# Two layers of attention and experts on one core: router logits and gate values of layer 1 projected in transposed form

## What is computed

```python
xn = layernorm(x)
logits = xn @ w_router            # 256 x 8; the two largest choose the experts
rw, sel = top_k(softmax(logits), 2); rw = rw / rw.sum()
low = xn @ Wg1                    # 256 x 16
gate = low @ Wg2                  # 16 x 256, later sigmoid(gate) scales the attention
q, k, v = silu(xn @ Wq), silu(xn @ Wk), silu(xn @ Wv)
```

## Time and profile before

| what | us |
|---|---|
| median of three runs | 997.73 |
| the three runs | 994.32, 997.73, 1004.47 |
| the profiled execution | 995.28 |
| its span in the profile | 993.4 |
| TensorE busy in the span | 837.8 (84%) |
| VectorE busy | 573.7 (58%) |
| ScalarE busy | 394.2 (40%) |
| POOL busy | 311.4 (31%) |

### The profile page before, as it was taken

How to read it: one execution, slowest core, us unless ns; L and a number is a source line. 1 busy time by engine, 2 the same in 40 slices (tenths; PEclk the granted TensorE clock), 3 DMA queues, 4 the chain that set the end, 5 groups by cost and what they waited for, 6 DMA issues and landing times. The chain is left out here.

```text
span 993.4 us, 14867 instructions
## 1 busy us (share of the span) xinstructions
PE 837.8 (84%) x4544; PEld 486.6 (49%) x4544; DVE 573.7 (58%) x1269; ACT 394.2 (40%) x676; POOL 311.4 (31%) x250
## 2 busy tenths in 40 slices
PE   4989999848998987997988748399799999999990
PEld 4765655501223443433434436256566666666660
DVE  7746877258779776777674435424343443444435
ACT  2336666414555565466446604022122222222220
POOL 3033567363001330151015113214243344344230
PEclk9999999956999997999798966599899999999995
DMA  8514655463222323533403301799773344344007
GB/s 273 136 59 146 198 184 183 151 187 92 86 67 61 117 85 100 170 106 107 145 27 107 127 21 61 213 288 307 209 171 99 92 125 115 90 116 124 23 16 259
DMA packets 158353, 130.26 MB, mean 131 GB/s; under 512 B 64128, under 2 KB 139920, under 8 KB 158288
## 3 DMA queue, kind: packets, MB, share of 16 engines
q1 hardware_dynamic: 151136, 109.89, 37.6%
q0 software_dynamic: 7152, 19.54, 6.7%
HBM read 83.37 MB, written 46.01 MB: 130 GB/s over the span
## 5 line engine op out<-in xcount | busy, mean ns | idle before, releaser
L1305 DVE TENSOR_REDUCE b_negmax<-b_psM 128x1 f32<-128x512 f32 x256 | 163.0, 683 | 61.0 <-PE b_psM L1491 58.2
L1242 ACT ACTIVATE b_probs<-b_psE 128x512 f32<-128x512 f32 x256 | 138.8, 594 | 125.9 <-PE b_psE L1509 125.1
L1491 PE MATMUL b_psM<-b_kst,b_qst 96*128 96x512 bf16 x256 | 98.5, 427 | 42.1 <-DVE b_negmax L1305 26.0
L1509 PE MATMUL b_psE<-b_qst,b_kst 98*128 98x512 bf16 x256 | 87.9, 405 | 14.1 <-ACT b_probs L1242 9.6
L2007 PE MATMUL d_psG<-d_w,d_xT 128*128 x156 | 76.9, 616 | 2.5 <-issue 1.4
L1860 POOL DMA_INDIRECT scratch_ys<-d_y,put x39 | 39.7, 1018 | 122.4 <-ACT d_y L1891 120.8
L2032 PE MATMUL d_psY<-d_w,d_hidden 128*128 x312 | 76.8, 390 | 0.8 <-ACT d_hidden L1885 0.8
L2015 PE MATMUL d_psU<-d_w,d_xT 128*128 x156 | 75.0, 603 | 0.0
L1491 PEld LDWEIGHTS b_psM<-b_kst,b_qst 96*128 96x128 bf16 x256 | 24.5, 99 | 101.4 <-DVE b_negmax L1305 76.7
L1518 PE MATMUL b_psV<-b_probs,b_vst 128*32 128x512 f32 x512 | 71.9, 634 | 2.5 <-ACT b_probs L1242 2.5
L1509 PEld LDWEIGHTS b_psE<-b_qst,b_kst 98*128 98x128 bf16 x256 | 20.4, 98 | 101.0 <-issue 51.8
(11 more groups left out here) (353 smaller groups left out, 1591.0 us busy)
## 6 DMA issues: line engine op xcount, KB each, us to landing
scratch_parts<-a_parts SPq DMA_DIRECT2D x12, 512.0 KB, 4.2
b_qst<-scratch_parts SPq DMA_DIRECT2D x96, 64.0 KB, 2.1
b_kst<-scratch_parts SPq DMA_DIRECT2D x96, 64.0 KB, 2.1
scratch_parts<-b_part SPq DMA_DIRECT2D x24, 256.0 KB, 3.1
d_qst<-scratch_parts SPq DMA_DIRECT2D x96, 64.0 KB
d_kst<-scratch_parts SPq DMA_DIRECT2D x96, 64.0 KB
scratch_ys<-a_y SPq DMA_DIRECT2D x39, 128.0 KB, 1.8
scratch_v<-a_xn SPq DMA_DIRECT2D x4, 1024.0 KB, 6.9
```

Source lines behind the costliest of these rows:

```text
L1242: nc.scalar.activation(probs[k % PSLOTS][:, h, :], psE[h % 2][:, :], ACT.Exp, scale=float(HD) ** -0.5).then_inc(scores_used[h % 2], 1)
L1305: nc.vector.tensor_reduce(negmax[i][:, t, h:h + 1], psM[:, h % 2, :], AX_X, ALU.max, negate=True).then_inc(rows_used[h % 2], 1)
L1491: nc.tensor.matmul(psM[:, h % 2, :], qst[g][0:STACK, h, t * P:(t + 1) * P], kst[g][0:STACK, h, :], start=True, stop=True).then_inc(rows_re ...
L1509: nc.tensor.matmul(psE[h % 2][:, :], kst[g][0:STACKM, h, k * P:(k + 1) * P], qst[g][0:STACKM, h, :], start=True, stop=True).then_inc(score ...
```

## The change

TensorE's `logits_low` becomes `project_low`: `wr` is now the stationary operand and xT moves, so that six products of 512 columns give a 24 x 512 tile: rows 0 to 15 are low, transposed, and rows 16 to 23 are the logits, transposed (in `wr` the two blocks of columns change places for that). VectorE copies the whole tile to lowT in slot 10. In slot 11 TensorE's `turn_logits` multiplies each tile of lowT by the 24 x 24 identity in ordinary fp32 products, which brings both back to rows; VectorE's `choose` reads the logits there. The choosing so moves from slot 10 to slot 11 on VectorE; `gap_exp` moves from slot 11 to behind `silu_half(1)` in slot 12 on ScalarE, and `route_weights` from the front of slot 12 to slot 13 behind `first_part` on VectorE. The copy and the transposes of low in rows are gone. The diff, whole but for blank lines:

```diff
--- before.py
+++ after.py
@@ -996,7 +996,7 @@
         half = sb("half", [P, KT, SEQ])
         parts = [sb(f"part{i}", [P, KT, SEQ], BF16) for i in range(3)]
         v32 = sb("v32", [P, TILES, HEADS, VW])
-        low, lowT, sg = sb("low", [P, TILES, HD]), sb("lowT", [HD, SEQ]), sb("sg", [P, TILES, D])
+        lowT, sg = sb("lowT", [RW, SEQ]), sb("sg", [P, TILES, D])
         qd, kd = sb("qd", [P, KT, SEQ]), sb("kd", [P, TILES, D])
         y0, y0_at, y0_wts = sb("y0", [P, 2 * TILES, D]), sb("y0_at", [P, 2, TILES], U32), sb("y0_wts", [P, 2, TILES])
         y0_held = sb("y0_held", [P, 1])
@@ -1030,8 +1030,8 @@
             sem(n) for n in ("half_ps", "half", "rest", "qd", "kd"))
         part_done = sems("part", 3)
         part_stored, stored = keep["part_stored"], keep["stored"]
-        low_ps, low_done, lowT_ps, lowT_done, gate_ps, gate_done, k_ps, v_ps, v_done = (
-            sem(n) for n in ("low_ps", "low", "lowT_ps", "lowT", "gate_ps", "gate", "k_ps", "v_ps", "v"))
+        low_ps, lowT_done, logits_ps, gate_ps, gate_done, k_ps, v_ps, v_done = (
+            sem(n) for n in ("low_ps", "lowT", "logits_ps", "gate_ps", "gate", "k_ps", "v_ps", "v"))
         y0_found, y0_in, y0_half, y0_added = sem("y0_found"), sem("y0_in"), sem("y0_half"), sem("y0_added")
         y0_free = sem("y0_free")
         LOADED = 16 * (2 * len(Q_PARTS) + 1)
@@ -1099,7 +1099,7 @@
                 sp.dma_start(dst, src).then_inc(consts_in, 16)
             routing.load(sp, io)
             for dst, src in ((rqk[:, :, 0:D], "Wq1"), (rqk[:, :, D:2 * D], "Wk1"), (rv, "Wv1"),
-                             (rr[:, :, 0:E], "router1"), (rr[:, :, E:RW], "Wg1"),
+                             (rr[:, :, HD:RW], "router1"), (rr[:, :, 0:HD], "Wg1"),
                              (wo[:, :, :], "Wo0")):
                 sp.dma_start(dst, io[src].rearrange("(k p) n -> p k n", p=P)).then_inc(weights_in, 16)
             sp.dma_start(wg2[:, :], io["Wg2"]).then_inc(weights_in, 16)
@@ -1293,8 +1293,8 @@
             act.wait_ge(padded, 1)
             for dst, src in ((wqk, rqk), (wv, rv), (wr, rr)):
                 nc.scalar.activation(dst[0][:, :, :], src[:, :, :], ACT.Copy).then_inc(w_hi, 1)
-            loop(act, attend, {4: (copy_combT,), 8: (copy_xT,), 9: (silu_half(0),), 10: (first_part,), 11: (second_part, gap_exp),
-                               12: (silu_half(1),), 14: (gate,), 15: (silu_v,)})
+            loop(act, attend, {4: (copy_combT,), 8: (copy_xT,), 9: (silu_half(0),), 10: (first_part,), 11: (second_part,),
+                               12: (silu_half(1), gap_exp), 14: (gate,), 15: (silu_v,)})
         @block.vector
         def _(dve):
@@ -1417,15 +1417,14 @@
                 dve.wait_ge(part_done[1], 2 * n + 2)
                 nc.vector.tensor_tensor(parts[2][:, :, :], half[:, :, :], parts[1][:, :, :], ALU.subtract).then_inc(part_done[2], 1)
-            def copy_low(n):
-                small = second(n)[:, 0, 0:TILES * RW].rearrange("p (t n) -> p t n", n=RW)
+            def copy_lowT(n):
                 dve.wait_ge(low_ps, n + 1)
-                nc.vector.tensor_copy(low[:, :, :], small[:, :, E:RW]).then_inc(low_done, 1)
-                routing.choose_pair(dve, n, small[:, :, 0:E], hot)
-
-            def copy_lowT(n):
-                dve.wait_ge(lowT_ps, n + 1)
-                nc.vector.tensor_copy(lowT[:, :], second(n)[0:HD, 1, :]).then_inc(lowT_done, 1)
+                nc.vector.tensor_copy(lowT[:, :], second(n)[0:RW, 0, :]).then_inc(lowT_done, 1)
+
+            def choose(n):
+                dve.wait_ge(logits_ps, n + 1)
+                small = second(n)[:, 1, 0:TILES * RW].rearrange("p (t n) -> p t n", n=RW)
+                routing.choose_pair(dve, n, small[:, :, HD:RW], hot)
             def route_weights(n):
                 routing.weigh_pair(dve, n, wts)
@@ -1476,8 +1475,8 @@
                     fold(t, 0)
             loop(dve, attend, {0: (weigh_terms(0),), 1: (weigh_terms(1),), 2: (weigh_terms(2),), 3: (weigh_terms(3),), 5: (residual,), 6: (moments,),
-                               7: (normalise, find_next), 8: (split_xT,), 9: (prepare,), 10: (copy_low, fold_next(0)), 11: (copy_lowT, fold_next(1)),
-                               12: (route_weights, fold_next(2), place), 13: (decay_k, first_part, fold_next(3), spread_ids),
+                               7: (normalise, find_next), 8: (split_xT,), 9: (prepare,), 10: (copy_lowT, fold_next(0)), 11: (choose, fold_next(1)),
+                               12: (fold_next(2), place), 13: (decay_k, first_part, route_weights, fold_next(3), spread_ids),
                                14: (second_part, spread_rows), 15: (third_part, finish_tables)}, ready)
         @block.tensor
@@ -1600,20 +1599,19 @@
                     mm.then_inc(half_ps, 1)
                 return step
-            def logits_low(n):
+            def project_low(n):
                 if not alone(n):
                     pe.wait_ge(half_done, 2 * n + 1)
+                mm = three(nc, second(n)[0:RW, 0, :], [(wr[0][:, k, :], wr[1][:, k, :], xT[0][:, k, :], xT[1][:, k, :])
+                                                       for k in range(KT)])
+                mm.then_inc(low_ps, 1)
+
+            def turn_logits(n):
+                pe.wait_ge(lowT_done, n + 1)
                 for t in range(TILES):
-                    c = slice(t * P, (t + 1) * P)
-                    mm = three(nc, second(n)[:, 0, t * RW:(t + 1) * RW],
-                               [(xT[0][:, k, c], xT[1][:, k, c], wr[0][:, k, :], wr[1][:, k, :]) for k in range(KT)])
-                mm.then_inc(low_ps, 1)
-
-            def turn_low(n):
-                pe.wait_ge(low_done, n + 1)
-                for t in range(TILES):
-                    mm = nc.tensor.transpose(second(n)[0:HD, 1, t * P:(t + 1) * P], low[:, t, :], ident[:, :])
-                mm.then_inc(lowT_ps, 1)
+                    mm = nc.tensor.matmul(second(n)[:, 1, t * RW:(t + 1) * RW], lowT[:, t * P:(t + 1) * P], ident[0:RW, 0:RW],
+                                          start=True, stop=True, skip_group_check=True)
+                mm.then_inc(logits_ps, 1)
             def project_gate(n):
                 pe.wait_ge(lowT_done, n + 1)
@@ -1621,7 +1619,7 @@
                 if not alone(n):
                     pe.wait_ge(kd_done, n + 1)
                 for t in range(TILES):
-                    mm = nc.tensor.matmul(second(n)[:, t // 2, (t % 2) * D:(t % 2 + 1) * D], lowT[:, t * P:(t + 1) * P],
+                    mm = nc.tensor.matmul(second(n)[:, t // 2, (t % 2) * D:(t % 2 + 1) * D], lowT[0:HD, t * P:(t + 1) * P],
                                           wg2[:, :], start=True, stop=True, skip_group_check=True)
                 mm.then_inc(gate_ps, 1)
@@ -1664,7 +1662,7 @@
                 pe.wait_ge(w_lo, 3)
             loop(pe, attend, {0: (heads(0),), 1: (heads(1),), 2: (heads(2),), 3: (heads(3),), 4: (turn_combined,), 5: (project_out,),
-                              8: (turn_x,), 9: (project_half(0),), 10: (logits_low,), 11: (turn_low,), 12: (project_half(1), rank),
+                              8: (turn_x,), 9: (project_half(0),), 10: (project_low,), 11: (turn_logits,), 12: (project_half(1), rank),
                               13: (turn_k,), 14: (project_gate,), 15: (project_v, invert)}, ready)
```

## The result

| | before | after |
|---|---|---|
| median of four runs, us | 1000.54 | 985.05 |
| the runs | 994.32 to 1004.47 | 983.53 to 987.60 |
| profiled execution / its span | 995.28 / 993.4 | 983.53 / 981.7 |
| ratio, 95% interval | | 0.9876 [0.9833, 0.9919] |

The change makes the kernel faster, by 12.4 us in 1000 by the ratio (8 to 17 by the interval) and by 15.5 by the two medians, where 4.0 were forecast. The sign was right; the size was not.

A forecast was written before the change was run, and what follows sets the result against it. In middle, a TensorE-VectorE round trip, the engine carrying a slot's side work is late: TensorE in slot 10, VectorE in slot 11. Gains 1.65 + 0.6 + 1.1 + 0.6 = 4.0 us; forecast 993.0 us, range 987.5 to 1000.

The forecast's parts named there:

- step 1: TensorE, slot 10: 24 small products (2.79 us) become six of 512 columns (1.43 us), a lead of 1.36 us.
- Steps 2 and 3: VectorE: choosing leaves slot 10 (1.5 us less before slot 11's reductions), enters slot 11 (+1.4), held there by POOL about 1.0.
- Step 5: SyncE, stores before slot 13's first cast: landing keeps nearly 2.65 us of lead in the first turn, 1.6 in the second.
- Step 6: VectorE, slot 13: route_weights, caught behind POOL's L1207 ahead of two folds, loses 1.0 us in each of the two turns.
- Batch 2: Products fall from 3.49 to 1.43 us; turning instructions cost 0.5 to 0.8 more, gap_exp 0.2: gain 1.1 us.
- Turn 2: Second turn of the loop in middle: lead 1.6 us at the landing less 1.0 for the weights, gain 0.6.
- Rival (c): Shorter side products leave the clock low in one more attention slot group per batch: 6 to 10 us, 1002; chance 0.08.
- Turn 1: First turn of the loop in middle: lead 2.65 us less 1.0 for the weights, gain 1.65.
- Tail: Batch 3's steps alone: ranking starts 2.0 us sooner, route_weights is held some 2.1 us; net gain 0.6 us.
- Rival (a): Lead is kept: choosing does not meet POOL, or small operations are not held; 8 us faster, 989; chance 0.17.
- Rival (b): VectorE becomes the late engine from slot 11 to 14; 2.6 us slower, 999.5; chance 0.15.

The follow-up runs named there:

- E3: Kernel before with only gap_exp and route_weights moved as in the change: 1013.98 us, ratio 1.0006.
- E4: Kernel before with its 24 products and transposes, but choosing moved to slot 11, gap_exp and route_weights moved as in the change: 1014.36 us, ratio 1.0006.
- E6: Kernel after with its six products in slot 10 made twice, same values into the same place: 993.18 us, ratio 0.9961.
- E5: Kernel after, unchanged, run again on a further chip: 987.18 us, ratio 0.9883.
- E7: Kernel after with the 24 short products, which nobody reads, also made in slot 10 behind the six: 1001.32 us, ratio 1.0034.
- E8: Kernel after with route_weights moved from slot 13 to slot 15, on the chip of E5: 986.72 us, ratio 0.9887.
- E1: Kernel before, unchanged, profiled once more: 1013.93 us, ratio 1.0006.
- E11: Kernel after with the 24 short products also made in slot 10, ahead of the six: 1003.49 us, ratio 1.0054.
- E2: Kernel after with route_weights moved from slot 13 to slot 15, on the chip of E1: 1004.1 us, ratio 0.9907.

## Why the prediction was right in kind and wrong in size

**The bound, and step 1: right.** TensorE was late in slot 10, and the six products saved 1.22 us there (forecast 1.36). E3 and E4 leave its time there and there is no gain; E6 brings it back, and half to two thirds of the gain go. The forecast was built on this time and the moved work alone; what else changed was the granted clock.

**Steps 2 and 3: right, with one other instruction held.** Slot 11's wait for the reductions is gone. The collision with POOL came, on L164, not on L168, and cost 0.66 us in turn 1 and 0.65 in turn 2, not 1.0, because both began later than forecast (359.29 and 359.92 for 357.3 and 357.7). In batch 2 it was held 1.60. In the tail L164 was held 1.88. The Trainium skill, "SBUF — State Buffer", section Who interferes with whom, has a VectorE operation with two inputs in SBUF wait for a POOL instruction that reads SBUF; the trace agrees: 0.83 to 1.88 us for L164, 0.17 without.

**Step 5: right about SyncE's start, short behind it.** SyncE's loads of slot 11 began 2.58 us earlier in both turns (forecast 2.65). What followed was not a fixed sequence. In turn 2 the two transfers of `send_max` stood closer. The queue's rows, before, then after:

```profile
459.61 0.29 SPq L1087 DMA_DIRECT2D scratch_max<-b_nmT  x1
461.91 0.25 SPq L1089 DMA_DIRECT2D b_qst<-scratch_max  x1
```

```profile
457.54 0.29 SPq L1087 DMA_DIRECT2D scratch_max<-b_nmT  x1
458.94 0.25 SPq L1089 DMA_DIRECT2D b_qst<-scratch_max  x1
```

The second waits for the first to land: 2.30 us before, 1.40 after, 0.9 more lead than the copy's 1.66 (forecast 1.6), and at the cast 2.56. Before, the first was issued 0.57 us behind the last load of group 2, after 1.49. The two go together in all fourteen profiles: the second follows the first by 2.18 to 2.48 us in the eight cases with 0.57, and by 1.29 to 1.80 in the twenty with 1.22 or more. That the loads are what slows it is argued, not tested. In turn 1 the parts were issued 3.62 us earlier, but from issue to cast they took 6.17 us for 4.40, so 1.85 were left (forecast 2.65). E5 repeats this (6.03); E6, E7 and E8 do not (4.4 to 4.6); E1, which is the kernel before, took 5.94. That term is as uncertain as a store's landing.

**Step 6: half the size.** 1.0 us forecast, 0.54 measured four times. I counted the held weight as new and did not take back that before, L1369 was held as long behind the same POOL operation (2.23 us there, 0.48 now). One hold took the place of another; what is left is roughly route_weights' own length.

**Batch 2: the term of the sum that the clock mis-sized, 1.1 forecast, 3.55 measured.** (Turn 2 is further off, but much of that lies in the profile of before.) I let the low clock stand, and so took the turning instructions at twice their time and everything behind at the old pace. The clock did not fall. Rival (c) had the mechanism, "it can as well be gained", but with a chance of 0.08 and priced only as a loss. Rows 8 and 9 showed the low clock at the 24 products and behind them; I took it for a property of the place, and E7 against E11 shows that it hangs on what TensorE does first there. That this accounts for the whole 2.4 us is not shown: in E6 the full clock in slots 10 and 11 was followed by a low stretch, and 3.13 of the 3.55 were gone.

**Turn 2: 0.6 forecast, 4.49 measured.** 0.9 is `send_max`, 0.45 the weights, about 2.2 the low stretch in the profile of before, the rest small. **Turn 1: 1.65 for 2.23**: 0.8 less at the cast, 0.46 less for the weights, 0.91 more from a shorter low stretch behind. **Tail: 0.6 for 1.19**: kd came 1.74 us sooner, a little more than the 1.3 to 1.6 said, and of the hold again only half was lost.

Without that stretch the sections give 9.3 us, as E1 and E2 do (8.6). The times themselves say more, 10.3 to 15.5 by the medians of the three pairs; the profiled execution of before, 995.28 us, was faster than that kernel's median on every chip, although it has the stretch. The chance of faster by over 1%, 0.09, was too low: no case of mine added the terms' high ends to a gained clock. Rival (a), 8 us, came nearer than the forecast, although its condition failed: the operations were held. Rival (b) did not come: the lead at the cast was over 1.0 in every section.

## What to carry to other kernels

When a change replaces the work that stands in front of a drop of the granted clock, price the stretch behind it at both levels, with a real chance for each. To see how much of a gain is an engine's time, put back as much time as was saved and no more. When a moved operation is caught by a lock, first see which operation was caught there before; only the difference is a cost. A saving that is passed on through a transfer should be tried with the wait for that transfer removed, since much of it may be had, and more, by buffers of their own for what waits.

## What was not expected of the hardware

- The same products in the other order changed the granted clock for some 7 us (0.50 against 1.00) and the section by 3.1 us.
- Of two operations of 4 columns that began beside one POOL subtraction, RECIPROCAL (0.18 us) went through and the fp32 copy L183 was held (1.80 for 0.17). MAX8 kept its length beside POOL too (L162, 0.37 for four, beside L1212 in turn 1), and so did FIND_INDEX8 (0.16, in the tail of before beside L1207).
- The eight instructions against the 24 x 24 identity took 1.07 us, 0.13 each, and the eight against 64 columns 1.00: between 24 and 64 columns the number of columns made no difference.
- One chip of three had a stall of some 6 us in slot 9 of both turns, of unknown cause, and was 1.5% slower with every kernel.
